# One decoder layer on one core: ScalarE writes the hidden layer's high part and full value, instead of ScalarE and VectorE in turn

## The chip, the cores and the metric

The kernel runs on 1 core of a Trainium2 chip. The time is device microseconds (µs) of one execution of the whole program. TensorE does the matrix products, ScalarE (ACT) the activations, VectorE (DVE) and GpSimd (POOL) elementwise work and reductions, SyncE (SP) issues the transfers.

## What is computed

For 16 batches of 256 tokens, each 256 wide: `x + attention(layernorm(x))` with 16 heads, then a cross attention to 77 context rows, then a soft mixture layer. All in float32. The mixture layer, which the change touches, is

```
logits   = xn @ se.T                     # 256 tokens x 1024 slots (8 experts x 128)
slots    = softmax over tokens (logits).T @ xn
h        = gelu(slots @ w1)              # 1024 slots x 1024 hidden, exact gelu
processed= h @ w2
out      = softmax over slots (logits) @ processed
```

## The kernel before

Products that need float32 accuracy are made of three products of rounded numbers (function `three`, lines 456 to 460): an operand is split into a high part, rounded to float32r, and a low part, the rest; the sum is hi·hi + lo·hi + hi·lo. So each intermediate result is split: as a rule ScalarE copies it out of PSUM rounded (`_hi`) and VectorE subtracts this from the same bank (`_lo`, `minus`, L1060).

The hidden layer is split in another way. Four chunks of 256 slots are worked one after the other in each batch; in a chunk TensorE makes four quarters (`hidden`, 12 products each, into one PSUM bank: banks 6 and 5 in turn, banks 1 to 4 in the last batch), ScalarE evaluates gelu of a quarter into the float32 tile `h_f` (`ge`, L1006), VectorE rounds it into `h_hi` (`hid`, L1278), and GpSimd subtracts: `h_lo = h_f - h_hi` (`hid` of its own, L1396). `h_lo` and `h_f` lie in the same memory, so the subtraction is in place. A quarter is 128x512 elements. The product with `w2` (`outer`, two halves of 24 products) of a chunk starts when the fourth `h_lo` is there. The semaphore `ge` is also what TensorE waits for before it writes the bank again: `hidden` of quarter 2 and 3, the transposes `lt` of the next chunk (bank 6), `slots` (bank 5).

A batch passes three stages, called c (self attention), d (cross attention) and m (mixture; l is the last chunk of the batch before). Each pass of the main loop holds c of batch b+2, d of b+1 and m of b. The order of the steps on each engine is written out by hand in lists of tokens such as `m.hidden.0.3` (stage, step, chunk, quarter): START, ORDER (the loop body, 13 passes, b = 1 to 13) and FINISH. An engine does its list strictly in order; semaphores tie the engines together. MISC and QUAD (with _START and _FINISH) say in which order the steps of c and d use PSUM bank 0 and banks 1 to 4. `idle` steps in START are products that nobody reads, put between waits.

Exp (`ed`, `ec`, `ex`, `ex2`) and gelu (`ge`) lie in different activation tables, so ScalarE loads a table whenever its list goes from one to the other. The copies need no load.

Steps named below: `mh2`, `xo`, `pr`, `cb`, `sl`, `ds` are ScalarE's copies out of PSUM; `mx` is VectorE's maximum over four banks (L1141), `sh` its mask subtraction, `nrm` its normalisation, `acc` its sum of the output (L1296), `edn` its normalisation of the dispatch weights. On TensorE `lt`, `dispatch`, `comb`, `mt`, `tr`, `ob` are transposes, `scores`, `shifted`, `pv` (L546, L566 with L570, L583) work on 32-row or 32-column parts of the array, `combine` and `slots` are products of the `three` kind.

Of the kernel before, what the change touches and what calls it, by code (L numbers as in the profile page):

```python
# [14 lines left out]
G, R, Q, C = 4, 4, 4, 2  # L15
# [73 lines left out]
        d0.scores2.1 d0.pv2.0 c1.k d0.mt2.1 c1.q d0.shifted2.1 d0.tr2.0 c1.v d0.ob2.0 c1.scores.0 d0.pv2.1 s1.idle.3
        d0.tr2.1 s1.idle.4 c1.mt.0 s1.idle.4 d0.ob2.1 c1.shifted.0 d0.oproj2 s1.idle.1 c1.scores.1 c1.pv.0 s1.idle.6  # L90
        c1.mt.1 s1.idle.5 c1.shifted.1 s1.idle.3 d0.xt.3 s1.idle.7 d0.logits.0 d0.logits.1 d0.logits.2 d0.logits.3
        s1.idle.3 m0.lt.0 c1.scores.2 c1.pv.1 s1.idle.6 c1.mt.2 s1.idle.2 m0.dispatch.0 c1.shifted.2 c1.tr.0
        m0.slots.0 c1.ob.0 c1.scores.3 c1.pv.2 m0.hidden.0.0 c1.mt.3 m0.hidden.0.1 c1.shifted.3 d1.kv m0.hidden.0.2
# [1465 lines left out]
```

## Time and profile before

| | |
|---|---|
| three runs | 1810.91, 1811.00, 1812.59 µs; median 1811.0 |
| profiled execution, its own time | 1810.3 µs |
| its span, first to last instruction | 1808.5 µs |
| TensorE busy | 1781.7 µs |
| VectorE busy | 1062.4 µs |
| ScalarE busy | 970.0 µs |
| GpSimd busy | 429.9 µs |

The profile is of one execution. Engine rows give busy time; a busy TensorE is one whose products overlap in its pipeline, so where exactly it loses time is read from the starts of its products in the timeline. A chain of waits is followed back from the last instruction. Times in the timeline count from the first instruction.

### The profile page before, as it was taken

What the parts mean: (1) busy time and instruction counts of PE and PEld (TensorE: products, weight loads), DVE (VectorE), ACT (ScalarE), POOL (GpSimd) and SP (SyncE); (2) the same over time, 40 slices, a digit from 0 to 9 for tenths busy, and PEclk for the clock granted to TensorE, in tenths of its full rate; (3) what the DMA queues carried; (4) which work ended last, traced back from release to release, by engine and by line L of the source; (5) the groups of instructions that cost most, each with busy time, mean ns of one, the idle gap of its engine ahead of it and who ended that gap; (6) DMA issues with size and microseconds to landing.
All of it is one profiled execution on the core that took longest, in us unless ns stands there. A gap on an engine that the chain in (4) does not pass through costs nothing.

```text
span 1808.5 us, 40567 instructions
## 1 busy us (share of the span) xinstructions
PE 1781.7 (99%) x17278; PEld 1596.0 (88%) x17278; DVE 1062.4 (59%) x2213; ACT 970.0 (54%) x1713; POOL 429.9 (24%) x351
## 2 busy tenths in 40 slices
...
DMA packets 20851, 19.65 MB, mean 11 GB/s; under 512 B 9921, under 2 KB 19777, under 8 KB 20289
## 3 DMA queue, kind: packets, MB, share of 16 engines
...
q14 instruction: 41, 0.33, 0.1%
...
## 4 chain that ended last, share of the span: by engine, by line
PE 91%; DVE 4%; POOL 3%; ACT 2%; issue 1%; DMA 0%; POOLq 0%; DVEq 0%; SPq 0%; ACTq 0%
PE ps L458 22%; PE ps L459 20%; PE ps L460 20%; PE ps L546 4%; PE ps L566 3%; POOL h_lo L1396 3%; PE ps L583 2%; PE ps L677 2%; PE ps L693 2%; PE ps L836 2%; PE ps L658 2%; PE ps L768 1%; PE ps L613 1%; PE ps L759 1%; PE ps L500 1%; DVE h_hi L1278 1%
## 5 line engine op out<-in xcount | busy, mean ns | idle before, releaser
L1396 POOL TENSOR_TENSOR h_lo<-h_f,h_hi 128x512 fp32r<-128x512 f32 x256 | 336.2, 1323 | 1125.8 <-DVE h_hi L1278 1125.8
L458 PE MATMUL ps<-w_hi,h_hi 128*128 128x256 f32 x1024 | 299.4, 292 | 6.4 <-POOL h_lo L1396 4.6
L458 PE MATMUL ps<-sl_hi,w_hi 128*128 128x256 f32 x1024 | 302.4, 295 | 1.9 <-DVE sl_lo L1060 1.5
L459 PE MATMUL ps<-w_hi,h_lo 128*128 128x256 f32 x1024 | 289.3, 283 | 0.0
L459 PE MATMUL ps<-sl_hi,w_lo 128*128 128x256 f32 x1024 | 289.2, 282 | 0.0
L460 PE MATMUL ps<-sl_lo,w_hi 128*128 128x256 f32 x1024 | 289.1, 282 | 0.0
L460 PE MATMUL ps<-w_lo,h_hi 128*128 128x256 f32 x1024 | 289.1, 282 | 0.0
L1006 ACT ACTIVATE h_f<-ps 128x512 f32<-128x512 f32 x256 | 149.4, 597 | 143.0 <-PE ps L460 142.4
L1278 DVE CAST h_hi<-h_f 128x512 fp32r<-128x512 f32 x256 | 156.7, 622 | 118.0 <-ACT h_f L1006 117.6
L458 PEld LDWEIGHTS ps<-w_hi,h_hi 128*128 128x128 f32 x1024 | 195.1, 191 | 21.5 <-POOL h_lo L1396 18.5
L458 PEld LDWEIGHTS ps<-sl_hi,w_hi 128*128 128x128 f32 x1024 | 195.0, 190 | 20.2 <-issue 10.5
L459 PEld LDWEIGHTS ps<-sl_hi,w_lo 128*128 128x128 f32 x1024 | 195.7, 191 | 0.1
L459 PEld LDWEIGHTS ps<-w_hi,h_lo 128*128 128x128 f32 x1024 | 195.5, 191 | 0.0
L460 PEld LDWEIGHTS ps<-sl_lo,w_hi 128*128 128x128 f32 x1024 | 195.5, 191 | 0.0
L460 PEld LDWEIGHTS ps<-w_lo,h_hi 128*128 128x128 f32 x1024 | 195.4, 191 | 0.0
L910 ACT ACTIVATE pt<-ps 128x2048 f32<-128x2048 f32 x64 | 120.4, 1881 | 81.5 <-PE ps L570 72.9
L1141 DVE TENSOR_REDUCE mx<-ps 128x8 f32<-128x2048 f32 x64 | 146.2, 2285 | 22.5 <-PE ps L546 22.4
L1060 DVE TENSOR_TENSOR ds_lo<-ps,ds_hi 128x512 fp32r<-128x512 f32 x64 | 44.1, 688 | 90.5 <-ACT ds_hi L879 90.4
L879 ACT ACTIVATE ds_hi<-ps 128x512 fp32r<-128x512 f32 x64 | 38.2, 597 | 104.3 <-PE ps L768 104.2
L970 ACT ACTIVATE edt<-ps,cm 128x256 f32<-128x256 f32 x128 | 59.6, 470 | 60.6 <-DVE cm L1257 58.9
L1006 ACT ACT_TABLE_LOAD x67 | 86.0, 1283 | 8.7 <-PE ps L460 7.6
L879 ACT ACTIVATE mh<-ps 128x512 fp32r<-128x512 f32 (+1 forms) x96 | 43.9, 457 | 77.8 <-PE ps L555 54.6
...
## 6 DMA issues: line engine op xcount, KB each, us to landing
...
```

What stands on the lines that cost most here:

```text
L458: te.matmul(o, lhs[0], rhs[0], start=first, stop=False)
L459: te.matmul(o, lhs[1], rhs[0], start=False, stop=False)
L460: return te.matmul(o, lhs[0], rhs[1], start=False, stop=last)
L546: last = te.matmul(ps[:, 1 + i, t * S:(t + 1) * S], q[rows, c, t * P:(t + 1) * P], km[rows, e, c, :], start=True, stop=True)
L566: te.matmul(ps[:, 1 + i, j * S:(j + 1) * S], km[rows, e, c, j * P:(j + 1) * P], q[rows, c, :], start=True, stop=False)
L879: return nc.scalar.activation(o, i, ACT.Copy)
L910: nc.scalar.activation(pt[:, :, :, :].rearrange("p i j s -> p i (j s)"), ps[:, 1:1 + R, :], ACT.Exp)\
L970: last = nc.scalar.activation(edt[:, e, :], ps[:, 6, e * S:(e + 1) * S], ACT.Exp, bias=cm[:, k:k + 1], accum_out=csum[:, k:k + 1])
L1006: nc.scalar.activation(h_f[:, 2 * q:2 * q + 2, :], halves(hidden_bank(b, q)), ACT.Gelu).then_inc(s["ge"], 1)
L1141: V.tensor_reduce(mx[:, n, :, :], ps[:, 1:1 + R, :].rearrange("p i (t s) -> p i t s", t=NT), AX, ALU.max, negate=True).then_inc(s["mx"], 1)
L1278: V.tensor_copy(h_hi[:, 2 * q:2 * q + 2, :], h_f[:, 2 * q:2 * q + 2, :]).then_inc(s["h_hi"], 1)
L1396: Q_.tensor_tensor(h_lo[:, part, :], h_f[:, part, :], h_hi[:, part, :].bitcast(f32), ALU.subtract)\
```

## The change

Three things. ScalarE's `ge` evaluates gelu twice from the same bank: first rounded into `h_hi`, then in full into `h_f`; `ge` is signalled by the second, `h_hi` by the first. VectorE's `hid` is gone. GpSimd's `hid` waits for both. The lists of START and ORDER, and MISC and MISC_START, are new; the lists of FINISH are as before, but VectorE's without `hid`. VectorE's `kv` waits in addition for `pv2` of the batch before.

```diff
             def ge(b, c, q):   # ScalarE
-                nc.scalar.activation(h_f[:, 2 * q:2 * q + 2, :], halves(hidden_bank(b, q)), ACT.Gelu).then_inc(s["ge"], 1)
+                part = slice(2 * q, 2 * q + 2)
+                nc.scalar.activation(h_hi[:, part, :], halves(hidden_bank(b, q)), ACT.Gelu).then_inc(s["h_hi"], 1)
+                nc.scalar.activation(h_f[:, part, :], halves(hidden_bank(b, q)), ACT.Gelu).then_inc(s["ge"], 1)
             def kv(a):         # VectorE
                 dve.wait_ge(s["kv_ps"], nth("kv_ps", a, 1))
+                if later(a):
+                    dve.wait_ge(s["pv2"], nth("pv2", a - 1, C))
-            def hid(b, c, q):  # VectorE
-                n = 4 * c + q
-                dve.wait_ge(s["ge"], nth("ge", b, n + 1))
-                V.tensor_copy(h_hi[:, 2 * q:2 * q + 2, :], h_f[:, 2 * q:2 * q + 2, :]).then_inc(s["h_hi"], 1)
             def hid(b, c, q):  # GpSimd
                 pool.wait_ge(s["h_hi"], nth("h_hi", b, 4 * c + q + 1))
+                pool.wait_ge(s["ge"], nth("ge", b, 4 * c + q + 1))
```

TensorE's list of the loop (ORDER), before and after:

```diff
-        m.lt.0 l.outer.3.0 d.kv m.dispatch.0 l.outer.3.1 c.xt.1 l.comb.3 m.slots.0 d.xt.2 c.k c.q m.hidden.0.0 d.q2
-        c.v m.hidden.0.1 d.scores2.0 m.hidden.0.2 m.hidden.0.3 d.mt2.0 m.lt.1 l.combine.3 d.shifted2.0 m.outer.0.0
-        m.dispatch.1 c.scores.0 d.pv2.0 m.comb.0 m.slots.1 m.outer.0.1 c.mt.0 m.hidden.1.0 c.shifted.0 m.hidden.1.1
-        d.tr2.0 d.scores2.1 c.pv.0 m.hidden.1.2 m.hidden.1.3 d.mt2.1 m.lt.2 m.combine.0 d.shifted2.1 d.ob2.0
-        m.outer.1.0 m.dispatch.2 c.scores.1 d.pv2.1 m.slots.2 m.comb.1 c.mt.1 m.outer.1.1 m.hidden.2.0 c.shifted.1
-        m.hidden.2.1 d.tr2.1 c.scores.2 m.combine.1 d.ob2.1 m.hidden.2.2 c.mt.2 m.hidden.2.3 m.lt.3 d.oproj2
-        c.shifted.2 c.pv.1 m.outer.2.0 c.tr.0 m.dispatch.3 c.scores.3 c.pv.2 m.slots.3 m.comb.2 c.mt.3 m.outer.2.1
-        d.xt.3 c.shifted.3 m.hidden.3.0 m.hidden.3.1 c.pv.3 d.logits.0 c.ob.0 m.hidden.3.2 m.hidden.3.3 c.tr.1
-        d.logits.1 d.logits.2 d.logits.3 c.ob.1 m.combine.2 c.oproj
+        m.lt.0 l.outer.3.0 d.kv m.dispatch.0 l.outer.3.1 c.xt.1 m.slots.0 l.comb.3 c.k d.xt.2 c.q m.hidden.0.0 d.q2
+        c.v m.hidden.0.1 d.scores2.0 m.hidden.0.2 m.hidden.0.3 d.mt2.0 m.lt.1 l.combine.3 d.shifted2.0 m.outer.0.0
+        m.dispatch.1 c.scores.0 d.pv2.0 m.slots.1 m.comb.0 c.mt.0 m.outer.0.1 c.shifted.0 m.hidden.1.0 m.hidden.1.1
+        d.tr2.0 d.scores2.1 c.pv.0 m.hidden.1.2 d.mt2.1 m.hidden.1.3 m.lt.2 m.combine.0 d.shifted2.1 m.outer.1.0
+        m.dispatch.2 c.scores.1 d.ob2.0 m.outer.1.1 c.mt.1 m.slots.2 m.comb.1 d.pv2.1 c.shifted.1 d.tr2.1
+        m.hidden.2.0 m.hidden.2.1 c.pv.1 c.scores.2 m.hidden.2.2 m.hidden.2.3 c.mt.2 m.lt.3 m.combine.1 c.tr.0
+        c.shifted.2 d.ob2.1 m.outer.2.0 m.dispatch.3 c.pv.2 c.scores.3 d.oproj2 m.slots.3 m.comb.2 c.mt.3 m.outer.2.1
+        c.ob.0 c.shifted.3 m.hidden.3.0 m.combine.2 m.hidden.3.1 d.xt.3 m.hidden.3.2 m.hidden.3.3 c.pv.3 d.logits.0
+        d.logits.1 c.tr.1 d.logits.2 c.ob.1 d.logits.3 c.oproj
```

ScalarE's list of the loop after:

```
        m.ed.0 m.ds.0 c.xt.1 l.cb.3 l.pr.3 m.sl.0 d.xt.2 d.q2 c.q m.ge.0.0 m.ge.0.1 m.ge.0.2 d.mh2.0 m.ge.0.3 m.ed.1
        d.ex2.0 m.ds.1 m.ec.0 d.xo2.0 m.sl.1 m.cb.0 c.mh.0 c.ex.0 m.ge.1.0 m.ge.1.1 c.xo.0 m.pr.0 m.ge.1.2 d.mh2.1
        m.ge.1.3 m.ed.2 d.ex2.1 m.ec.1 m.ds.2 d.od2.0 c.mh.1 m.cb.1 m.sl.2 d.xo2.1 c.ex.1 m.ge.2.0 c.xo.1 m.ge.2.1
        m.pr.1 m.ge.2.2 c.mh.2 m.ge.2.3 m.ed.3 c.ex.2 m.ec.2 d.od2.1 m.ds.3 c.xo.2 m.sl.3 m.cb.2 c.mh.3 m.pr.2 c.od.0
        c.ex.3 m.ge.3.0 m.ge.3.1 d.xt.3 m.ge.3.2 m.ge.3.3 c.xo.3 m.ec.3 d.logits.0 d.logits.1 c.od.1 d.logits.2
        d.logits.3
```

In both versions this list loads a table eight times in a pass (four times to gelu, four times back). VectorE's list of the loop after has, around the steps spoken of below, `c.k m.row_max c.v d.mx2.0`, `c.mx.0 m.sl.1 m.cb.0 c.sh.0` and `m.cm.3 c.sh.2 c.nrm.0 m.acc.1 m.edn.3`. Through the whole program the new ScalarE list changes table 129 times, the old one 135 times; the difference lies in START. START has 184 idle products after and 183 before.

## Rows read from the trace of the kernel before

**Rows 1.** The page, part 1: busy time, share, instructions of each engine.
```profile
PE 1781.7 (99%) x17278; PEld 1596.0 (88%) x17278; DVE 1062.4 (59%) x2213; ACT 970.0 (54%) x1713; POOL 429.9 (24%) x351
```

**Rows 2.** Busy time by stage: start:end, length, busy (instructions) by engine, PE clock.
```profile
0.00:233.00 233.00, 220.70 (x2194) 187.39 (x2195) 124.60 (x261) 117.65 (x188) 46.85 (x43) 1.00 0.12 35
341.10:449.10 108.00, 107.86 (x1057) 96.75 (x1056) 65.43 (x137) 59.21 (x105) 25.96 (x21) 1.00 0.03 7
1637.80:1808.50 170.70, 158.05 (x1357) 150.50 (x1355) 87.27 (x171) 82.16 (x160) 45.14 (x35) 1.00 0.02 6
```

**Rows 3.** Chain that ended last: start, length, what (same place, first and last pass).
```profile
308.86 2.64 POOL h_lo L1396 x2
...
1605.60 2.64 POOL h_lo L1396 x2
```

**Rows 4.** Waits of TensorE's weight loads in 233 to 1638: total, times, longest.
```profile
PEld ps L458 <- POOL h_lo L1396: 12.0, 26, 0.6
```

**Rows 5.** The page, part 5: groups, busy and mean, idle before and releaser.
```profile
L1396 POOL TENSOR_TENSOR h_lo<-h_f,h_hi 128x512 fp32r<-128x512 f32 x256 | 336.2, 1323 | 1125.8 <-DVE h_hi L1278 1125.8
...
L1006 ACT ACTIVATE h_f<-ps 128x512 f32<-128x512 f32 x256 | 149.4, 597 | 143.0 <-PE ps L460 142.4
L1278 DVE CAST h_hi<-h_f 128x512 fp32r<-128x512 f32 x256 | 156.7, 622 | 118.0 <-ACT h_f L1006 117.6
...
L1006 ACT ACT_TABLE_LOAD x67 | 86.0, 1283 | 8.7 <-PE ps L460 7.6
```

**Rows 6.** Tile h_hi: VectorE's rounding, duration min/median/max in ns.
```profile
L1278 DVE CAST h_hi<-h_f x256: 411/427/1427, 133.7 to 1791.7; 128x512 fp32r<-128x512 f32 x128
```

**Rows 7.** Timeline of TensorE in a pass of the loop: start, length, what.
```profile
846.91 0.29 PE L460 MATMUL ps<-sl_lo,w_hi 128*128 128x256 f32 x1
847.03 0.60 PE L759 MATMUL ps<-consts,lg 128*128 128x128 f32 x4
...
850.60 1.07 PE L583 MATMUL ps<-pt,vz 128*32 128x256 f32 x16
851.82 0.39 PE L458 MATMUL ps<-w_hi,h_hi 128*128 128x256 f32 x1
...
856.84 1.07 PE L583 MATMUL ps<-pt,vz 128*32 128x256 f32 x16
857.84 0.39 PE L458 MATMUL ps<-ds_hi,xs_hi 128*128 128x256 f32 x1
...
864.35 0.48 PE L570 MATMUL ps<-sh,ones 32*128 32x256 f32 x4
864.76 0.39 PE L458 MATMUL ps<-sl_hi,w_hi 128*128 128x256 f32 x1
```

**Rows 8.** Timeline of ScalarE, the same pass and the program's end.
```profile
832.90 0.60 ACT L879 ACTIVATE sl_hi<-ps 128x512 fp32r<-128x512 f32 x1 [0.99 <-PE ps L460]
...
842.37 1.09 ACT L1006 ACTIVATE h_f<-ps 128x512 f32<-128x512 f32 x2
...
847.23 0.60 ACT L1006 ACTIVATE h_f<-ps 128x512 f32<-128x512 f32 x1 [0.57 <-PE ps L460]
...
1791.02 0.60 ACT L1006 ACTIVATE h_f<-ps 128x512 f32<-128x512 f32 x1 [0.84 <-PE ps L460]
```

**Rows 9.** Timeline of VectorE, the same pass.
```profile
842.34 2.29 DVE L1141 TENSOR_REDUCE mx<-ps 128x8 f32<-128x2048 f32 x1 [0.33 <-PE ps L546]
...
846.61 0.82 DVE L1278 CAST h_hi<-h_f 128x512 fp32r<-128x512 f32 x1
```

**Rows 10.** Timeline of GpSimd, the same pass and the program's end.
```profile
845.85 1.30 POOL L1396 TENSOR_TENSOR h_lo<-h_f,h_hi 128x512 fp32r<-128x512 f32 x1 [20.30 <-DVE h_hi L1278]
847.51 1.27 POOL L1396 TENSOR_TENSOR h_lo<-h_f,h_hi 128x512 fp32r<-128x512 f32 x1 [0.36 <-DVE h_hi L1278]
...
1791.65 2.79 POOL L1396 TENSOR_TENSOR h_lo<-h_f,h_hi 128x512 fp32r<-128x512 f32 x2 [0.36 <-DVE h_hi L1278]
```

**Rows 11.** Timeline of TensorE at the program's end.
```profile
1794.48 0.39 PE L458 MATMUL ps<-w_hi,h_hi 128*128 128x256 f32 x1 [2.07 <-POOL h_lo L1396]
```

More of the change, by code:

```diff
@@ L89 @@
[L89 to L93, printed above, removed]
@@ L94 @@
-        s1.idle.1 c1.pv.3 s1.idle.2 c1.tr.1 m0.hidden.0.3 c1.ob.1 m0.lt.1 c1.oproj m0.outer.0.0 m0.dispatch.1 d1.xt.2
-        m0.outer.0.1 c2.xt.1 m0.slots.1 m0.comb.0 c2.k c2.q c2.v m0.hidden.1.0 c2.scores.0 d1.q2 m0.hidden.1.1
-        c2.mt.0 m0.hidden.1.2 c2.shifted.0 m0.hidden.1.3 d1.scores2.0 c2.pv.0 m0.lt.2 d1.mt2.0 m0.combine.0
-        d1.shifted2.0 m0.outer.1.0 m0.dispatch.2 d1.scores2.1 d1.pv2.0 m0.outer.1.1 d1.mt2.1 m0.slots.2 m0.comb.1
-        d1.shifted2.1 d1.tr2.0 m0.hidden.2.0 d1.ob2.0 c2.scores.1 m0.hidden.2.1 m0.hidden.2.2 c2.mt.1 m0.hidden.2.3
@@ L99 @@
-        d1.pv2.1 c2.shifted.1 m0.lt.3 d1.tr2.1 m0.combine.1 d1.ob2.1 c2.scores.2 c2.pv.1 m0.dispatch.3 d1.oproj2
-        m0.comb.2 c2.mt.2 m0.slots.3 c2.shifted.2 m0.outer.2.0 c2.tr.0 c2.scores.3 c2.pv.2 m0.outer.2.1 c2.mt.3
-        m0.hidden.3.0 c2.shifted.3 d1.xt.3 m0.hidden.3.1 m0.hidden.3.2 m0.combine.2 c2.pv.3 d1.logits.0 c2.ob.0
-        m0.hidden.3.3 c2.tr.1 d1.logits.1 d1.logits.2 c2.ob.1 d1.logits.3 c2.oproj
+        s0.idle.1 s0.se_transp.0.0 s0.idle.3 c0.mt.2 s0.idle.4 c0.shifted.2 c0.tr.0 s0.idle.3 c0.ob.0 s0.idle.1
@@ new lines @@
+        c0.scores.3 c0.pv.2 s0.se_transp.0.1 s0.idle.4 c0.mt.3 s0.idle.4 c0.shifted.3 s0.idle.8 c0.pv.3 s0.idle.2
+        c0.tr.1 s0.se_transp.1.0 s0.idle.2 c0.ob.1 s0.idle.2 c0.oproj s0.idle.3 d0.kv s0.idle.8 d0.xt.2 s0.idle.5
+        d0.q2 s0.se_transp.1.1 s0.idle.2 d0.scores2.0 c1.xt.1 s0.idle.6 d0.mt2.0 c1.k d0.shifted2.0 s0.idle.8
+        d0.scores2.1 d0.pv2.0 s0.idle.3 d0.mt2.1 c1.q d0.shifted2.1 d0.tr2.0 c1.v c1.scores.0 d0.pv2.1 s1.idle.3
+        d0.ob2.0 s1.idle.2 c1.mt.0 s1.idle.4 c1.shifted.0 d0.tr2.1 s1.idle.3 d0.ob2.1 s1.idle.1 c1.scores.1 d0.oproj2
@@ new lines @@
+        s1.idle.5 c1.mt.1 s1.idle.6 c1.pv.0 s1.idle.4 d0.xt.3 c1.shifted.1 d1.kv d0.logits.0 d0.logits.1 d0.logits.2
+        d0.logits.3 s1.idle.3 c1.scores.2 c1.pv.1 m0.lt.0 s1.idle.4 c1.mt.2 s1.idle.4 c1.shifted.2 c1.tr.0
+        m0.dispatch.0 s1.idle.2 c1.ob.0 s1.idle.1 c1.scores.3 c1.pv.2 m0.slots.0 c1.mt.3 s1.idle.4 c1.shifted.3
+        m0.hidden.0.0 s1.idle.2 c1.pv.3 m0.hidden.0.1 c1.tr.1 m0.hidden.0.2 c1.ob.1 m0.hidden.0.3 c1.oproj m0.lt.1
+        m0.outer.0.0 m0.dispatch.1 m0.outer.0.1 c2.xt.1 m0.slots.1 c2.k c2.q c2.v d1.xt.2 m0.comb.0 c2.scores.0 d1.q2
@@ new lines @@
+        m0.hidden.1.0 c2.mt.0 c2.shifted.0 m0.hidden.1.1 m0.combine.0 d1.scores2.0 m0.hidden.1.2 d1.mt2.0
+        m0.hidden.1.3 m0.lt.2 d1.shifted2.0 c2.pv.0 m0.outer.1.0 d1.scores2.1 d1.pv2.0 m0.dispatch.2 d1.mt2.1
+        m0.comb.1 d1.shifted2.1 d1.tr2.0 m0.slots.2 d1.ob2.0 c2.scores.1 d1.pv2.1 m0.outer.1.1 c2.mt.1 m0.hidden.2.0
+        c2.shifted.1 m0.combine.1 d1.tr2.1 c2.scores.2 c2.pv.1 m0.hidden.2.1 m0.hidden.2.2 c2.mt.2 m0.hidden.2.3
+        d1.ob2.1 c2.shifted.2 d1.oproj2 m0.lt.3 m0.outer.2.0 c2.scores.3 m0.dispatch.3 c2.tr.0 m0.outer.2.1 c2.mt.3
@@ L103 @@
+        m0.slots.3 m0.comb.2 c2.pv.2 c2.shifted.3 d1.xt.3 m0.hidden.3.0 m0.combine.2 d1.logits.0 c2.ob.0
+        m0.hidden.3.1 m0.hidden.3.2 c2.pv.3 d1.logits.1 d1.logits.2 c2.tr.1 m0.hidden.3.3 c2.ob.1 d1.logits.3
+        c2.oproj
     """,
     act="""
-        c0.xt.1 s0.hi.0 s0.hi.1 c0.q c0.mh.0 c0.ex.0 s0.se_squares c0.xo.0 c0.mh.1 c0.ex.1 c0.xo.1 s0.hi.2 c0.mh.2
-        s0.hi.3 c0.ex.2 c0.od.0 s0.se_hi.0.0 c0.xo.2 c0.mh.3 c0.ex.3 s0.se_hi.0.1 c0.xo.3 s0.hi.4 c0.od.1
-        s0.se_hi.1.0 d0.xt.2 s0.se_hi.1.1 d0.q2 d0.mh2.0 d0.ex2.0 c1.xt.1 d0.xo2.0 d0.mh2.1 c1.q d0.ex2.1 d0.od2.0
@@ L187 @@
 MISC = """
-    d.kv c.xt1 d.xt2 d.q2 d.mt2.0 d.pv2.0 c.mt.0 d.tr2.0 c.pv.0 d.mt2.1 d.ob2.0 d.pv2.1 c.mt.1 d.tr2.1 d.ob2.1 c.mt.2
-    d.oproj2 c.pv.1 c.tr.0 c.pv.2 c.mt.3 d.xt3 c.pv.3 c.ob.0 c.tr.1 c.ob.1 c.oproj
+    d.kv c.xt1 d.xt2 d.q2 d.mt2.0 d.pv2.0 c.mt.0 d.tr2.0 c.pv.0 d.mt2.1 d.ob2.0 c.mt.1 d.pv2.1 d.tr2.1 c.pv.1 c.mt.2
+    c.tr.0 d.ob2.1 c.pv.2 d.oproj2 c.mt.3 c.ob.0 d.xt3 c.pv.3 c.tr.1 c.ob.1 c.oproj
 """.split()
```

100 lines of the change are left out of this document (44 added, 56 removed).

## The prediction

> **What bounds the kernel now.** I read the page's busy times first: TensorE 1781.7 of 1808.5 µs, ScalarE 970.0, VectorE 1062.4, GpSimd 429.9 [rows 1]. Busy time of overlapping products proves little, so next the stages and the chain. In the span's middle TensorE is busy 107.86 of 108.00 µs at clock 1.00, while at the start it lacks 12.3 of 233 µs and at the end 12.6 of 170.7 [rows 2]. The loop body repeats with a period of (1605.60 - 308.86) / 12 = 108.06 µs [rows 3], 13 times, 1404.8 µs of 1808.5. So the question is what 108.06 becomes, and then what the two ends become.
>
> GpSimd's 1125.8 µs of waiting for VectorE's rounding [rows 5] is the largest wait of the profile and costs almost nothing: TensorE's weight loads wait for `h_lo` 12.0 µs in 26 pieces over the 13 passes, two a pass [rows 4], and much of that lies behind products still in the array. What TensorE really loses is seen in its starts. A `pv` (16 L583) takes 1.00 from its start to the next step's when nothing is waited for (856.84 to 857.84), and 1.22 where `outer.2.0` follows (850.60 to 851.82) [rows 7]: 0.22 µs. `outer.1.0` loses 0.15 in the same way. That is 0.37 a pass, 4.8 in all, and all that the split of the hidden layer costs the loop.
>
> **Why that wait is there.** ScalarE has evaluated two quarters at 843.46 (842.37 + 1.09) [rows 8]; VectorE is in `mx` for 2.29 µs [rows 9], so GpSimd starts at 845.85 only, and its next one at 847.51: 1.66 apart though one takes 1.30 [rows 10]. The rounding between them is stretched to 0.82 [rows 9] against 0.41 undisturbed, and up to 1.43 [rows 6]. The Trainium skill has the reason ("SBUF — State Buffer", section "SBUF: two separate sides"): VectorE in a fast mode and GpSimd take a shared port pair as an exclusive lock. The rows agree (0.41 alone, up to 1.43 beside GpSimd). By that rule GpSimd's remaining subtractions still block VectorE's other fast operations, now at other moments.
>
> **The change part by part.**
>
> *VectorE's rounding goes.* 256 x 0.622 µs = 156.7 [rows 5], 8 to 10 µs of each pass's 65.43 [rows 2]. VectorE bounds nothing there, so this is worth nothing directly.
>
> *ScalarE evaluates twice.* Two evaluations back to back take 1.09, one 0.60 [rows 8], so the second costs 0.49. A rounded output costs the same as a plain one (`sl_hi` 0.60) [rows 8]. 16 x 0.49 = 7.8 µs a pass: 59.2 [rows 2] becomes 67.0, 62% of the pass; over the program 256 x 0.49 = 125. It bounds nothing on average either. No table load is added: both are gelu, and 67 loads of 1.28 [rows 5] stay or become a few less. Below: if the pair doesn't overlap it is 0.60, 9.6 a pass.
>
> *The way from a landed quarter to `h_lo`.* Before: 0.60, rounding 0.41 to 1.43 behind VectorE's queue, then GpSimd 1.30. After: 1.09, then 1.30, without VectorE. Alone that is 2.4 against 2.3 or more; its worth is that nothing of VectorE's queue stands in it, and that GpSimd's subtractions follow at 1.30, not 1.66. On the other hand `ge`, for which TensorE waits before it uses the bank again, comes 0.49 later, and all that stands behind `ge` in ScalarE's queue comes later by 0.49 for each quarter: `mh2`, `pr`, the table load ahead of `ed`.
>
> *The added wait of `kv` for `pv2`* looks back over more than 40 µs of the list (`pv2.1` stands in the middle of the pass, `kv` near the next one's start). It is free.
>
> *The new list of TensorE.* It has the same 90 steps. The steps cost the same wherever they stand, but the joints between them don't. From the last product of a step to the first of the next: 0.12 between full products and on to transposes (846.91 to 847.03), about 0.3 to 0.4 out of a 32-row step (0.41 over the last half's four short ones, 864.35 to 864.76) [rows 7]. Over the timeline each kind of joint repeats to 0.01: transposes to products 0.03, to transposes 0.11, to 32-row steps 0.20; products to 32-row steps 0.21; out of `scores` 0.30, of `pv` 0.31, of `shifted` 0.39; out of the projections `oproj` 0.22 to transposes, 0.31 to 32-row steps, 0.03 to products. Summed with these prices, the old list takes 107.42 without any wait. The pass takes 108.06; 0.37 are the waits above and 0.27 are hundredths spread over 90 joints. The new list changes 30-odd joints. Those that don't cancel: `oproj2` is followed by products, no longer by `shifted` (-0.28); two fewer transposes after transposes and one fewer 32-row step after them, for products after them (-0.36); two joints transposes to `pv` (+0.40, taken at 0.20 like the nearest, transposes to `scores`; between 0.11 and 0.31). With the small ones the new list sums to 107.05, range 106.9 to 107.3. Saved: 0.37.
>
> *Waits in the new loop.* I placed each chunk on the new list (µs from the pass's start, no waits; a quarter reaches ScalarE 0.32 after its last product starts, 846.91 to 847.23 [rows 7, 8]).
> Chunk 0: `hidden.0.2` is due at 20.94 and waits for `ge.0.0`, which stands behind `q2` and `q` (until 18.5), a table load (19.8) and its pair (20.95): 0.1 lost or none. `hidden.0.3`'s last product starts at 23.78; `mh2.0` stands ahead of `ge.0.3` and ends at 25.1, the pair at 26.2, GpSimd at 27.5; `outer.0.0` is due at 27.59. Nothing lost, 0.1 to spare.
> Chunk 1: `h_lo` at 51.3, due 51.90. Chunk 2: `h_lo` at 75.5, due 76.42; but `acc.1`, behind `sh.2` and `nrm.0` on VectorE, ends at 76.5: 0.1 lost. Chunk 3: `h_lo` at 100.4, due in the next pass.
> In sum 0.2 in place of 0.37. The other tight spots (2 µs between `hidden.c.2` and `lt`, a pair is through after 1.4) hold.
>
> The period: 107.05 + 0.27 + 0.2 = 107.5, against 108.06: -0.55, times 13 = -7.2 µs. Bounds: 107.2 (no waits) and 108.5 (0.25 lost at each of four chunks and the joints at their dear end): -11 to +6.
>
> *START.* Here latency of one batch's chain sets the time, and idle products fill it (184, before 183); QUAD_START, which orders that chain through banks 1 to 4, is unchanged. By prices the list is 0.3 shorter. The waits in it, 12.3 µs of TensorE not busy and more behind fillers [rows 2], fall elsewhere. Six table loads of 1.28 go [rows 5], off TensorE's path mostly. I take 0, bounds -4 and +4.
>
> *FINISH.* TensorE's and ScalarE's lists are the same, with 32 second evaluations in ScalarE's: 15.7 µs. At the very end it helps: the last evaluation starts 1791.02 [rows 8], its pair ends 1792.1, GpSimd is free and ends at 1793.5; before, its last two end at 1794.44 [rows 10], and `outer.3.0` starts 1794.48 after 2.07 idle [rows 11]. Gain 0.95. In chunks 0 to 2 of the last batch `ds` and `sl` stand behind one to three pairs, and reach TensorE 0.5 to 1.5 later; part of it goes into waits for `h_lo` already there. I take +0.5 for each of three, less 0.2 at the batch before. FINISH: +0.4; bounds -2 and +5.
>
> Sum: -7.2 + 0 + 0.4 = -6.8 on the profiled execution's own 1810.3 (span 1808.5 and 1.8 around it): 1803.5. The runs' median, 1811.0, is 0.7 above that execution: 1804.
>
> **Rivals.**
> *A, slower: ScalarE's queue becomes the wait in the loop.* The place is the gelu block of each chunk: table load, four pairs, and copies between them for which TensorE waits next. For it: only 0.1 is to spare at `outer.0.0` and none at `hidden.0.2`; at 0.60 for the second evaluation four pairs are 0.44 later. Against: 38% of ScalarE's pass remains idle. It decides when the waits exceed 1.1 a pass, 0.27 a chunk. At 1.6 a pass (0.4 a chunk) the period is 108.9: +11, and 1822. A page speaks for it: the Trainium skill ("ScalarE: Activation LUTs", section "Rules for kernel authors") gives plain elementwise work to VectorE, since it is faster there per element; the rows agree in size, 0.41 on VectorE and 0.49 on ScalarE. It would matter if ScalarE bounded.
> *B, no change: the joints don't pay.* The loop keeps new waits of 0.7 a pass and ends at 108.0; 1810 to 1811. For it: my prices come from one order, and the old list too had two tight spots.
> *C, faster by more.* No waits in the loop, and START gains 4: 13 x -0.85 - 4 = -15, 1796.
> *D, the change doesn't do what it says:* ScalarE would reload a table between the two evaluations, or the rounded one would be slower. Both are gelu, `sl_hi` shows the rounded form at full speed; 1 in 100.
>
> **How the numbers follow.** Forecast (1801 to 1807) 0.50, C 0.13, B 0.22, A 0.14, D 0.01. A measurement tells about 0.2%, 3.6 µs, from no change, so faster means below 1807.4, slower above 1814.6. Faster: forecast and C and a little of B, 0.65. Same: most of B and some of A, 0.21. Slower: 0.14. The range for 8 in 10 is 1796 to 1813; the likeliest case's own is 1801 to 1807.
>
> **What would show it.** The period by `outer.2.0` in successive passes: 107.5 (right), 108.0 (B), over 108.6 (A). GpSimd's subtractions back to back at 1.30, none 1.66 apart. ScalarE's pairs at 1.09 and about 67 µs busy in a pass, VectorE about 56. `outer.1.0` and `outer.2.0` without loss. TensorE's starts at the new joints: transposes to `pv` 0.20, `oproj2` to `slots` 0.03. At the end `outer.3.0` 1 µs sooner after its `combine.2`. I'd be wrong if START moved by more than 4 either way, or if `ds` and `sl` in the last batch cost over 1 µs each.

## The result, and the profile after

The changed kernel takes 1818.1 µs (median of 6 runs, 1817.1 to 1818.9) against 1811.0: ratio 1.0037, interval 1.0024 to 1.005. I had forecast a faster kernel, 1804 µs with a range of 1796 to 1813; the measured one is slower, and its time lies outside the range.

The profiled execution takes 1817.69 µs, of which the span is 1815.9. Line numbers of the changed kernel are 2 to 5 lower than those of the rows before (`h_lo` L1396 is L1392). The page's first part, as [rows 1]:

```profile
PE 1784.8 (98%) x17280; PEld 1599.7 (88%) x17280; DVE 942.8 (52%) x1957; ACT 1084.5 (60%) x1963; POOL 423.0 (23%) x351
```

VectorE lost 119.6 µs of work and ScalarE gained 114.5. Neither tells where the added 7.4 µs of span come from. The stages do, in the columns of [rows 2]:

```profile
0.00:242.40 242.40, 224.50 (x2197) 190.57 (x2198) 122.22 (x245) 117.44 (x198) 46.86 (x43) 0.98 0.11 34
350.20:458.20 108.00, 108.00 (x1059) 96.95 (x1058) 57.95 (x121) 66.92 (x121) 25.59 (x21) 1.00 0.03 7
1644.30:1815.90 171.60, 158.43 (x1357) 150.53 (x1355) 65.79 (x139) 96.70 (x192) 43.69 (x35) 0.99 0.02 6
```

The first and the last of these are START and FINISH; the bounds are the first product of the first loop pass and the first one after the last pass, in TensorE's timeline:

```profile
242.39 0.38 PE L755 MATMUL ps<-consts,lg 128*128 128x128 f32 x2
...
1644.28 0.38 PE L755 MATMUL ps<-consts,lg 128*128 128x128 f32 x2
```

A pass is (1644.28 - 242.39) / 13 = 107.84 µs. In the table, START runs from TensorE's first product of all (at 3.70 µs before, at 3.87 changed) to the first one of the loop; the whole is the median of the runs.

| kernel | START | a pass | FINISH | span | whole |
|---|---|---|---|---|---|
| before | 229.3 | 108.06 | 170.7 | 1808.5 | 1811.0 |
| changed | 238.5 | 107.84 | 171.6 | 1815.9 | 1818.1 |
| difference | +9.2 | -0.22 (13: -2.9) | +0.9 | +7.4 | +7.1 |

The three stages give +7.2; the span has 0.2 more since the first product itself comes 0.17 later. The loop did gain, less than forecast. START lost three times what the loop gained, and the first row above shows that TensorE's clock is no longer 1.00 there. Ten-microsecond stretches of START in the changed kernel, same columns:

```profile
60.00:70.00 10.00, 6.39 (x52) 5.84 (x50) 8.99 (x20) 1.44 (x3) 6.00 (x4) 0.96 0.16 38
70.00:80.00 10.00, 7.85 (x65) 7.52 (x66) 7.25 (x7) 0.60 (x1) 2.46 (x2) 0.53 0.01 2
80.00:90.00 10.00, 9.86 (x128) 8.21 (x126) 5.47 (x9) 4.33 (x5) 0.00 (x0) 1.00 0.01 2
```

TensorE is without work from 67.3 to 72.2 µs, and the clock granted from 70 to 80 is 0.53, about half. The timelines of the three engines there, changed kernel:

```profile
65.39 1.28 POOL L1385 TENSOR_TENSOR x<-x,biases 128x512 f32<-128x512 f32 x1
66.64 4.55 POOL L1423 TENSOR_TENSOR w_lo<-g_w,w_hi 128x2048 fp32r<-128x2048 f32 x1
71.42 1.27 POOL L1385 TENSOR_TENSOR x<-x,biases 128x512 f32<-128x512 f32 x1 [0.23 <-DVE xh_a L1104]
...
65.46 5.88 DVE L1104 TENSOR_SCALAR xh_a<-x,mv,pw 128x256 f32<-128x256 f32 x2
71.26 0.74 DVE L1349 SCALAR_TENSOR_TENSOR se_lo<-ps,gxs,se_hi 128x512 fp32r<-128x512 f32 x1
71.92 3.04 DVE L1335 SCALAR_TENSOR_TENSOR w_lo<-g_w,gam,w_hi 128x1024 fp32r<-128x1024 f32 x2
...
72.15 0.87 PE L853 MATMUL ps<-consts,g_se 128*128 128x128 f32 x3 [4.89 <-DVE se_lo L1349]
```

And the kernel before, GpSimd and VectorE:

```profile
55.88 4.53 POOL L1427 TENSOR_TENSOR w_lo<-g_w,w_hi 128x2048 fp32r<-128x2048 f32 x1 [18.15 <-ACT w_hi L879]
...
63.50 0.74 DVE L1354 SCALAR_TENSOR_TENSOR se_lo<-ps,gxs,se_hi 128x512 fp32r<-128x512 f32 x1
...
71.41 0.73 DVE L1106 TENSOR_SCALAR xh_a<-x,mv,pw 128x256 f32<-128x256 f32 x2
```

Read from the bottom up. TensorE waits 4.89 µs for `se_lo`. `se_lo` is queued on VectorE behind `c1.xh.1`, whose two `xh_a` instructions take 5.88 µs instead of 0.73, and end (71.34) just after GpSimd's `w_lo` ends (71.19). That is step `s0.lo.4`, w2's low part: the new GpSimd list has it behind `d0.bias.2`; in the old one it ran 10.8 µs earlier, and no VectorE instruction beside it took longer than it does alone. ScalarE's rounding of w2 and this subtraction moved, and have nothing to do with gelu. That the one holds up the other is so far only read from where they end; the runs below test it.

### The profile page after: what moved, and what is told of

It reads as the page before. It is cut to its first block, busy times and chain, and to the rows that moved or that the text cites. A ratio compares the mean times of both kernels' runs of the same rounds, so it can differ in the third digit from the quotient of the medians.

```text
span 1815.9 us, 40836 instructions
## 1 busy us (share of the span) xinstructions
PE 1784.8 (98%) x17280; PEld 1599.7 (88%) x17280; DVE 942.8 (52%) x1957; ACT 1084.5 (60%) x1963; POOL 423.0 (23%) x351
## 4 chain that ended last, share of the span: by engine, by line
PE 94%; DVE 2%; ACT 2%; POOL 1%; issue 1%; DMA 0%; POOLq 0%; DVEq 0%; SPq 0%; ACTq 0%
PE ps L454 21%; PE ps L455 20%; PE ps L456 20%; PE ps L562 4%; PE ps L542 4%; PE ps L579 3%; PE ps L673 2%; PE ps L689 2%; PE ps L719 2%; PE ps L654 2%; PE ps L764 1%; PE ps L609 1%; PE ps L755 1%; PE ps L832 1%; PE ps L496 1%; PE ps L861 1%
## 5 line engine op out<-in xcount | busy, mean ns | idle before, releaser
L1392 POOL TENSOR_TENSOR h_lo<-h_f,h_hi 128x512 fp32r<-128x512 f32 x256 | 330.8, 1300 | 939.3 <-ACT h_f L1004 938.4
L1003 ACT ACTIVATE h_hi<-ps 128x512 fp32r<-128x512 f32 x256 | 153.5, 600 | 63.9 <-PE ps L456 63.2
L1004 ACT ACTIVATE h_f<-ps 128x512 f32<-128x512 f32 x256 | 153.7, 600 | 0.0
L1375 POOL TENSOR_TENSOR pw_d<-ve_d,consts 128x2 f32<-128x2 f32 (+1 forms) x32 | 27.5, 859 | 264.8 <-DVE ve_d L1082 264.8
```

Source lines behind the costliest of these rows:

```text
L1003: nc.scalar.activation(h_hi[:, part, :], halves(hidden_bank(b, q)), ACT.Gelu).then_inc(s["h_hi"], 1)
L1004: nc.scalar.activation(h_f[:, part, :], halves(hidden_bank(b, q)), ACT.Gelu).then_inc(s["ge"], 1)
L1392: Q_.tensor_tensor(h_lo[:, part, :], h_f[:, part, :], h_hi[:, part, :].bitcast(f32), ALU.subtract)\
```

## The experiments

**Theory:** GpSimd's moved subtraction holds VectorE's `xh_a`, TensorE starves, its clock falls; this is START's loss. **Rivals:** the new START order is longer by itself; the second evaluation is what START pays for; in the loop and in FINISH, ScalarE's queue.

START repeats within 1.2 µs between kernels that have the same START (229.3, 229.1, 228.1 for the old order and split; 232.7, 232.4, 232.3 for that of run 1), so single tenths of it are not read. Part of that is there early: `d0.xt.2` starts 59.6 to 60.2 µs after TensorE's first product in kernels that are alike up to it. Waits are idle times of TensorE as the timeline gives them in brackets.

### 1. w2's low part back at its old place
```
POOL  - c0.bias.1 d0.rstd.2 c1.rstd.1 d0.bias.2 s0.lo.4 c1.bias.1
      + c0.bias.1 s0.lo.4 d0.rstd.2 c1.rstd.1 d0.bias.2 c1.bias.1
ACT   - c0.xo.3 s0.se_hi.1.0 c0.od.1 s0.hi.4
      + c0.xo.3 s0.hi.4 s0.se_hi.1.0 c0.od.1
```


> The changed kernel with one step of START put back where it stood before: GpSimd's subtraction for w2's low part (s0.lo.4) ahead of d0.rstd.2 instead of behind d0.bias.2, and ScalarE's rounding of w2 (s0.hi.4), which feeds it, ahead of s0.se_hi.1.0. Everything else is the changed kernel. Theory 1 (the 9.4 us that START lost come from that subtraction: it now runs at 66.64 to 71.19 beside VectorE's xh_a at 65.46, which takes 5.88 us instead of 0.73, TensorE then waits 4.89 us for se_transp.1.1 and works the next 10 us at a granted clock of 0.53): xh_a takes 0.7 us again, no idle time of TensorE of over 1 us between 60 and 90 us, granted clock 1.00 there, m.lt.0 of the first loop pass starts at about 234 instead of 242.39, and the whole takes 1809.5 us (1808.5 to 1811). Rival (the new START order is longer by itself, whatever GpSimd does): at least 1814 us. In between would mean that both have a part.

Measured: 1811.7 µs (1810.6 to 1812.4), ratio to before 1.0001 (0.9993 to 1.001); START 232.7, a pass 107.83. GpSimd and VectorE in this kernel:

```profile
66.12 1.28 POOL L1385 TENSOR_TENSOR x<-x,biases 128x512 f32<-128x512 f32 x1
...
66.19 1.69 DVE L1104 TENSOR_SCALAR xh_a<-x,mv,pw 128x256 f32<-128x256 f32 x2
```

Two steps moved back, the subtraction (it now runs at 56.26 to 60.78) and the rounding that feeds it, return 5.8 µs of START and 6.4 of the whole. The clock in 70 to 80 µs is 1.00. `xh_a` is still 1.69, not 0.7: it now meets GpSimd's `x += bias`, 1.28 µs, and waits for that one. The time is above the theory's 1808.5 to 1811 and below the rival's 1814: both have a part, and START is still 3.4 above the kernel before. Which of the two moves did it this run can't tell; run 2 leaves both where the changed kernel has them, and changes the subtraction alone.

### 2. The same subtraction in four pieces, at its new place
```
-  Q_.tensor_tensor(low, src, hi.bitcast(f32), ALU.subtract)
+  for k in range(4): Q_.tensor_tensor(low[:, 2*k:2*k+2, :], ...)
```


> The changed kernel with its orders untouched; GpSimd's subtraction for w2's low part is issued as four of 128x512 (of some 1.3 us each by the 128x512 ones of the trace) instead of one of 128x2048 (4.55 us). Theory 1 (a GpSimd elementwise instruction holds VectorE's fast fp32 forms off for as long as it runs, and lets them in where it ends): xh_a beside it takes 1.3 to 3.5 us instead of 5.88, se_transp.1.1 waits 2.5 to 4.5 us less, START is 2 to 5 us shorter than the 238.5 of the changed kernel, the whole 1813 to 1816 us. Rival 1 (VectorE waits for the whole of GpSimd's work on w2, by a semaphore or by buffers): xh_a still 5.9 us, or longer as four pieces cost more than one, the whole 1818 to 1819 us. Rival 2 (a loss of bandwidth instead of a lock: xh_a is slow for as long as GpSimd moves data): again 5.9 us or more.

Measured: 1815.8 µs, START 236.3 (-2.2). VectorE and GpSimd:

```profile
65.67 2.64 DVE L1104 TENSOR_SCALAR xh_a<-x,mv,pw 128x256 f32<-128x256 f32 x2
68.24 0.74 DVE L1349 SCALAR_TENSOR_TENSOR se_lo<-ps,gxs,se_hi 128x512 fp32r<-128x512 f32 x1
68.90 3.83 DVE L1335 SCALAR_TENSOR_TENSOR w_lo<-g_w,gam,w_hi 128x1024 fp32r<-128x1024 f32 x2
...
66.84 7.01 POOL L1425 TENSOR_TENSOR w_lo<-g_w,w_hi 128x512 fp32r<-128x512 f32 x4
```

The first `xh_a` ends behind `x += bias`, the second behind the first piece: 2.64 instead of 5.88. So VectorE is held for one GpSimd instruction at a time. The price comes after: the four pieces take 7.01 instead of 4.55, and VectorE's own `w_lo`, with two operands in SBUF, 3.83 instead of 3.04. `se_transp.1.1` waits 1.65 for `se_lo`, 3.2 less, and `d0.mt2.0` behind it waits 2.44 more. START, the whole and `xh_a` lie where the theory put them; neither rival's values came.

### 3. Fillers in the wait
```
PE  - d0.q2 s0.se_transp.1.1 s0.idle.2
    + d0.q2 s0.idle.24 s0.se_transp.1.1 s0.idle.2
```


> The changed kernel with 24 idle products (each a 128x128 by 128x128 product into a spare bank, as START has them everywhere) put between d0.q2 and s0.se_transp.1.1, so that TensorE works through the time in which it now waits for se_lo. VectorE's 5.88 us xh_a stays. Theory 1 as for e1, in two parts: some 5 us are the wait and some 3.3 us are the half clock after it. Filling the wait keeps the clock up, so the products of 72 to 79.5 us run at full speed: 1815 us (1814 to 1816), granted clock of 70 to 80 us at 0.9 or more. Rival 1 (the clock falls there for another reason than the idle time): 1818 us, clock still about 0.53. Rival 2 (the products themselves are late): 1818 us or more.

Measured: 1817.3 µs (1816.0 to 1817.6), START 237.9. The time is not the 1814 to 1816 that I expected. The granted clock is:

```profile
70.00:80.00 10.00, 9.36 (x109) 8.76 (x110) 8.53 (x9) 1.78 (x3) 3.07 (x2) 1.00 0.00 1
```

With work in the wait the clock stays at 1.00, so it was the idle time that brought it down. But of the 3.3 µs that I had expected from it only 1.7 are seen at `c1.x1` (VectorE's `x` at 145.42, changed kernel 147.12), and 0.6 at START's end. The fillers overran the wait by 0.3, and at `c2.xt.1` TensorE is idle 0.91 behind a load of `x`, 4.18 µs on its way; that the idle products already in the list absorbed the rest is my reading. This execution was also 0.6 late before the first filler (`d0.xt.2` at 64.04 instead of 63.47). So the half clock is worth 0.6 to 2.3 µs; START's own spread of 1.2 allows no closer value. Most of the 5.8 is the wait (4.89 before `se_transp.1.1`, 0.70 in run 1).

### 4. `se_lo` ahead of `xh_a` on VectorE
```
DVE - c1.stats.1 d0.xt.2 c1.xh.1 s0.se_lo.1.0 s0.lo.3
    + c1.stats.1 d0.xt.2 s0.se_lo.1.0 c1.xh.1 s0.lo.3
```


> The changed kernel with one swap in VectorE's START order: s0.se_lo.1.0 (0.74 us, reads PSUM) ahead of c1.xh.1 (the xh_a that takes 5.88 us beside GpSimd's 4.55 us subtraction). GpSimd's order and its subtraction at 66.64 to 71.19 stay. Theory 1 (GpSimd's instruction holds off only the fast form on SBUF operands, as xh_a has it, and TensorE suffered since se_lo was queued behind it): se_lo takes 0.7 us at about 65.5, se_transp.1.1 waits under 0.3 us, no fall of the clock, START 233 to 235 us (238.5 in the changed kernel), the whole 1812 to 1814. Rival 1 (every VectorE instruction is slow beside it): se_lo takes 4 us or more, the wait stays, 1818. Rival 2 (xh_a, now later, makes c1.xt.1 late instead): START 237 or more.

Measured: 1817.4 µs, START 238.6. VectorE, GpSimd, TensorE:

```profile
65.38 0.74 DVE L1349 SCALAR_TENSOR_TENSOR se_lo<-ps,gxs,se_hi 128x512 fp32r<-128x512 f32 x1
66.04 5.34 DVE L1104 TENSOR_SCALAR xh_a<-x,mv,pw 128x256 f32<-128x256 f32 x2
...
65.41 1.29 POOL L1385 TENSOR_TENSOR x<-x,biases 128x512 f32<-128x512 f32 x1
66.65 4.57 POOL L1423 TENSOR_TENSOR w_lo<-g_w,w_hi 128x2048 fp32r<-128x2048 f32 x1
...
71.52 0.63 PE L496 MATMUL ps<-consts,xh_a 128*128 128x128 f32 x4 [2.00 <-DVE xh_a L1104]
...
76.99 1.11 PE L663 MATMUL ps<-consts,md 128*128 128x128 f32 x4 [2.85 <-DVE xa_lo L1058]
```

Rival 2 is right on the time, theory 1 on the mechanism. `se_lo`, which reads PSUM, takes 0.74 beside GpSimd's `x += bias`; `xh_a` is held until 71.38, 0.15 after `w_lo` ends. The wait moved on to the transposes of `xh_a` and to `md`, in the same size (2.00 and 2.85 against 4.89), and the clock with it (0.63 in 70 to 80 µs). VectorE's whole chain is 5 µs late; swapping inside it doesn't help.

### 5. The old START order, double evaluation kept
START and MISC_START of the kernel before, less VectorE's `hid` steps; the rest is the changed kernel.

> The changed kernel (gelu evaluated twice, new loop and FINISH orders) with the START orders of the kernel before on all four engines, less VectorE's rounding steps. Theory 1 (START's order lost 9.4 us, the loop gained 2.9, FINISH lost 0.9): START takes 229 to 230 us as before, the loop 107.84 a pass, the whole 1808.7 us (1807.5 to 1810). Rival (the second gelu evaluation in START, 12 of 0.49 us on ScalarE, is what moved START): START at 232 us or more and the whole at least 1811 us.

Measured: 1810.6 µs, ratio 0.9997 (0.9988 to 1.0006); START 231.0, a pass 107.84, span 1808.2. START is between the theory's 230 and the rival's 232, and the whole is above the theory's 1807.5 to 1810: under the old order the double evaluation costs START 1.7 (230.5 in run 6, so 1.2 by that one), seen as waits before `d1.mt2.0` and `d1.scores2.0` (0.90 and 0.65, before 0.30 and 0.35).

### 6. The split alone, under all the old orders
The changed functions; START, ORDER, FINISH and MISC of the kernel before, less `hid`.

> The changed functions alone (gelu twice on ScalarE, no rounding on VectorE) under all the orders of the kernel before, less VectorE's rounding steps. It tells what the double evaluation is worth without any reordering. Theory 1 (TensorE stays the bound, the pass only loses small waits): START 229 to 230 us, a loop pass between 107.7 and 108.1, FINISH between 170.7 and 173, the whole 1807 to 1812 us. Rival (the doubled gelu of 0.5 us more a pair delays ScalarE's copies where the order was made for single ones, so that the reordering was needed): a loop pass of 108.5 us or more, and the whole at 1816 us or more.

Measured: 1822.6 µs, ratio 1.0062 (1.0049 to 1.0074); START 230.5, a pass 108.77, FINISH 171.6. The rival holds: without the new order the double evaluation makes a pass 0.71 longer. A pass in this kernel:

```profile
348.35:457.12 108.77, 108.41 (x1059) 96.85 (x1058) 57.06 (x122) 66.58 (x121) 25.23 (x22) 1.00 0.03 7
```

### 7. The new loop order with the old split
The functions of the kernel before, its START and FINISH; ORDER and MISC new, VectorE's 16 `hid` steps put in by hand (`... c.v m.hid.0.0 d.mx2.0 m.hid.0.1 m.hid.0.2 d.sh2.0 m.hid.0.3 m.cm.1 ...`).

> The loop orders of the changed kernel with the functions of the kernel before (one gelu a quarter on ScalarE, VectorE rounds it), VectorE's 16 rounding steps put by hand into its new order where their gelu ends; START and FINISH as in the kernel before. With the old order and the double evaluation a pass took 108.77 us, with both new 107.84, with both old 108.06. Theory 1 (the new order is better by itself, the double evaluation costs something on ScalarE in either order): a pass of 107.8 or less, the whole 1809 us or less. Rival (the new order only works since VectorE has the 13 us a pass free): 108.3 us or more a pass and 1814 us or more; a place of mine that is badly chosen would look the same, and shows as one large wait for h_lo or for a VectorE step in the pass.

Measured: 1833.9 µs, ratio 1.0126 (1.0112 to 1.014); a pass 109.81. TensorE in a pass:

```profile
859.85 0.39 PE L458 MATMUL ps<-w_hi,h_hi 128*128 128x256 f32 x1 [0.66 <-POOL h_lo L1398]
```

This wait for `h_lo` is in every pass (8.6 µs in 13), as are waits for VectorE's `sh` and `on` (4.4 each). That is what the rival and a badly chosen place both look like, and the run doesn't part them. Together with run 6: old order and old split 108.06, old order and double evaluation 108.77, both new 107.84. So the double evaluation needs the new order. Whether the new order needs the double evaluation stays open: the 109.81 may be my placing.

### 8. A third evaluation, in the loop
```
+  if 0 < b < B - 2: nc.scalar.activation(scr[q % 2], halves(hidden_bank(b, q)), ACT.Gelu)
```
on top of run 1, between the other two, into a spare tile.

> The first experiment (changed kernel with w2's low part at its old place) with a third gelu evaluation of each quarter from the same bank into a spare tile, in the 13 passes of the loop alone: 16 times 0.49 us, 7.8 us more of ScalarE a pass (from 66.9 to 74.8 of 107.8). It doubles the cost that the change adds. Theory (ScalarE's latency already sets some of the waits of a pass, with the changed order tuned for two): a pass 0.5 to 1.5 us longer than 107.84, the waits before outer.0.0 to outer.3.0 and before the products behind ScalarE's copies, the whole 1818 to 1831. Rival 1 (ScalarE has slack, as its busy share of 62% suggests; TensorE covers it): a pass 107.9 or less, the whole 1812.5 or less. Rival 2 (ScalarE becomes the chain): 3 us or more a pass, 1850 or more.

Measured: 1831.5 µs; a pass 109.37 (+1.54) for 7.1 µs more of ScalarE:

```profile
342.00:451.37 109.37, 108.43 (x1058) 96.95 (x1057) 56.60 (x121) 74.00 (x138) 25.68 (x21) 1.00 0.03 7
```

The growth is just above the theory's 0.5 to 1.5, and far from both rivals. The waits are before `hidden.0.2` (for `h_f`, 6.2 µs in the 13 passes) and for `h_lo` before `outer.0.0` (5.6). ScalarE, busy 62% of a pass, has no free slack in this order: each microsecond more of it costs 0.2 here, and cost 0.1 under the old order in run 6 (0.71 for 7.4). No order made for three evaluations was tried.

### 9. GpSimd's bias step away from `h_lo`
In the loop `d.bias.2` ahead of `m.hid.1.0` instead of ahead of `m.hid.2.3`, on top of run 1.

> The first experiment (w2's low part back at its old place) and one more move, in the loop: GpSimd's x += bias for the cross attention (d.bias.2, 1.28 us) ahead of m.hid.1.0 instead of between m.hid.2.2 and m.hid.2.3, where the product outer.2.0 waits 0.13 us behind it. Theory 1 (of the 0.34 us a pass that the forecast missed, 0.13 are this wait): a pass of 107.70 instead of 107.84, the whole 1.7 us below the first experiment, 1810 us. Rival (the wait is for ScalarE's pair in any case, or the bias step now meets a VectorE instruction and holds it): 107.84 or more a pass, 1811.7 us or more.

Measured: 1811.7 µs, a pass 107.86. It gained nothing: the rival's time, though for neither of its reasons. GpSimd, VectorE and TensorE in this kernel:

```profile
957.82 1.27 POOL L1392 TENSOR_TENSOR h_lo<-h_f,h_hi 128x512 fp32r<-128x512 f32 x1 [0.66 <-ACT h_f L1004]
...
959.31 0.68 DVE L1291 TENSOR_TENSOR acc<-ps,acc 128x512 f32<-128x512 f32 x1
...
960.13 0.36 PE L454 MATMUL ps<-w_hi,h_hi 128*128 128x256 f32 x1
```

The last `h_lo` is there 1.04 before `outer.2.0` starts (0.50 before it in the changed kernel), and the product still starts 0.16 after the last one of `d.ob2.1`, where this joint has 0.03 without a wait. `outer` waits for VectorE's `acc` as well, and `acc.1` ends 0.15 before `outer.2.0` starts, in both kernels and in each of the passes 4, 7 and 11. So the 0.13 are a wait for `acc.1`, as the prediction had it for chunk 2 (0.1). This is read from the code and the starts; no run moved `acc.1`.

### 10. Steps moved in START and FINISH
On top of run 9.

```
ACT START   c2.mh.0 c2.ex.0 m0.ec.1        (was m0.ec.1 c2.mh.0 c2.ex.0)
PE  START   m0.hidden.1.3 d1.mt2.0         (was d1.mt2.0 m0.hidden.1.3)
ACT FINISH  ds.1, sl.2, ds.3, pr.1, sl.3 ahead of gelu pairs
```


> As the one with d.bias.2 moved, and with five more steps moved, after the waits of the changed kernel. START: ScalarE's c2.mh.0 and c2.ex.0 ahead of m0.ec.1 (0.97 us, behind which c2.shifted.0 waits 1.09), TensorE's m0.hidden.1.3 ahead of d1.mt2.0 (which waits 1.28). FINISH: for the last batch ScalarE's copies ds.1, sl.2, ds.3, pr.1, sl.3 ahead of gelu pairs (slots.1 waits 1.40, hidden.2.0 0.94, slots.3 0.59, hidden.3.0 0.58). Theory (each of these waits is ScalarE's queue, not a chain that moves along): START 2 us less, FINISH 1.5 to 2.5 us less, the whole 1806 us (1805 to 1808). Rival (the waits return at the next product that needs the delayed gelu): FINISH within 0.5 us of 171.6, the whole 1809 us or more.

Measured: 1812.2 µs; START 233.7 (232.4 in run 9), FINISH 171.6. The rival holds for FINISH. `slots.1` waits 0.25 instead of 1.24, and in exchange there are waits before `comb.0` (0.52), `outer.1.0` (0.97) and `outer.2.0` (1.31) of which the changed kernel has none over 0.25. In the last batch a turn in ScalarE's queue is paid by a later product. START got no shorter either: `c2.shifted.0` still waits 0.99, and `hidden.1.2` now waits 1.08 and `d1.shifted2.0` 1.03.

### 11. Double evaluation in the loop alone
`ge` evaluates twice only for batches 1 to 13; START and FINISH are those of the kernel before with VectorE's `hid`; ORDER and MISC are new.

> Double evaluation and new order only in the 13 passes of the loop; START and FINISH with the orders of the kernel before and with its split (one gelu a quarter, VectorE rounds). Theory (the stages add up: START 229.3 and FINISH 170.7 as before, a pass 107.84): span 1805.6 us, 2.9 below the kernel before, the whole 1808 us (1807 to 1809.5) against 1811, ratio 0.9984. The double evaluation then costs 1.6 us in START and 0.9 in FINISH, which is what the kernel with the old START order showed. Rival (at the seams the loop's new order meets a state that the old START leaves, and gives back some of it): 1810 us or more, a first pass longer than 108 us.

Measured: 1807.5 µs (1806.8 to 1808.7), against 1810.6 for the kernel before in the same session: ratio 0.9985 (0.9976 to 0.9994), span 1805.6:

```profile
0.00:232.80 232.80, 220.48 (x2195) 187.12 (x2196) 125.68 (x261) 117.68 (x188) 46.90 (x43) 1.00 0.11 35
340.60:448.45 107.85, 107.85 (x1057) 96.82 (x1056) 57.94 (x121) 66.97 (x121) 25.61 (x21) 1.00 0.03 7
1634.80:1805.60 170.80, 158.02 (x1357) 150.49 (x1355) 88.31 (x171) 82.15 (x160) 44.91 (x35) 0.99 0.02 6
```

The stages add up to the forecast 1805.6: the two ends as before [rows 2], the loop as changed. This version is faster than the kernel before by 3 µs, and than the changed one by 10.

### 12. The new START order with the old split
Run 11 with the START of run 1, the 16 rounding steps of batch 0 put in by hand.

> As the one with the double evaluation in the loop alone, but with the new START order (w2's low part at its old place), with VectorE's 16 rounding steps of the first batch put by hand into it. It tells apart what of START's remaining 3.4 us (232.7 in the first experiment against 229.3) is the order and what the double evaluation, which cost 1.6 us under the old order. Theory 1 (the new START order is longer by itself): START 231 to 233 us. Rival (it is the double evaluation): START 229 to 230 us, the whole as the mixed kernel. A badly chosen place of a rounding step would show as a wait for h_lo of over 0.5 us at an outer product of batch 0.

Measured: 1813.3 µs, START 234.6, of which two waits are of my placing (`outer.0.0` 1.34, in run 1 0.30; `c2.ob.1` 1.50, there none): 232.1 without them, by subtraction and not by a run. But the two largest waits that run 1 has in START from 70 µs on are here too, with one evaluation: `c2.shifted.0` 0.99 (run 1: 0.99) and `d1.mt2.0` 1.45 (1.12); the kernel before has 0.30 or less at both. They come with the order, also without the second evaluation. That speaks for the order being longer by itself; by how much isn't settled.

**START's 9.2 µs in sum.** 5.8 for w2's low part (run 1). The other 3.4 are the second evaluation and the new order, and their shares are no better known than START repeats: 1.7 and 1.7 if the second evaluation costs what it did under the old order (run 5), 0.6 and 2.8 by run 12. Beside the two waits just named, run 1 has 0.70 before `se_transp.1.1` and 0.84 before `d0.mt2.0`, both behind VectorE; the kernel before has no such wait at either. No run took any of these waits away by itself.

## Why the prediction was wrong

**START at 0, bounds -4 to +4: this is the step that failed, and it decides the sign.** "Idle products fill it", I wrote, and "the waits in it ... fall elsewhere", without walking the new lists of GpSimd, VectorE and ScalarE. It measured +9.2, more than twice my upper bound. The fillers that I trusted are a fixed number between two steps; they cover no wait that wasn't there when they were counted. The prediction even wrote, with the Trainium skill ("SBUF — State Buffer", section "SBUF: two separate sides"), that GpSimd's subtractions would block VectorE's fast operations "at other moments", and then put no price on it. It thought of the 1.3 µs ones only. The longest GpSimd instruction of the kernel, 4.53 µs, was in the trace, and its step had moved in GpSimd's list. That section of the Trainium skill calls the pair an exclusive lock for a whole instruction; the rows agree: the two `xh_a` take 0.73 alone, 1.69 beside 1.28, 2.64 beside 1.28 and a piece of 1.33, 5.88 beside 1.28 and 4.55 one after the other.

**The loop: right in direction, 0.22 instead of 0.55 a pass, so 2.9 µs of gain instead of 7.2.** ScalarE's pairs took 1.09 as forecast, its pass 66.9 (67), VectorE's 57.95 (56), and GpSimd's subtractions follow the pairs. In the page's groups:

```profile
L1392 POOL TENSOR_TENSOR h_lo<-h_f,h_hi 128x512 fp32r<-128x512 f32 x256 | 330.8, 1300 | 939.3 <-ACT h_f L1004 938.4
...
L1003 ACT ACTIVATE h_hi<-ps 128x512 fp32r<-128x512 f32 x256 | 153.5, 600 | 63.9 <-PE ps L456 63.2
...
L1004 ACT ACTIVATE h_f<-ps 128x512 f32<-128x512 f32 x256 | 153.7, 600 | 0.0
```

The weight loads' waits for `h_lo` fell from 12.0 in 26 [rows 4] to:

```profile
PEld ps L454 <- ACT h_f L1004: 5.4, 13, 0.4
...
PEld ps L454 <- POOL h_lo L1392: 3.9, 13, 0.3
```

The first is `hidden.0.2` behind `ge.0.0`, foreseen at 0.1 or none: most of it lies behind products in the array, and the product starts 0.05 later than with single evaluation in the same order (run 7). With 0.13 at `outer.2.0` (run 9), and 0.03 or less at two more, the waits are 0.2 a pass, as I had them.

**What failed in the loop is the sentence "The steps cost the same wherever they stand".** The timeline of TensorE, cut into steps by the lists, gives for all 90 (medians of 11 passes, so the sums can miss a pass by 0.01):

| kernel | steps, first to last product | joints, waits in them | a pass |
|---|---|---|---|
| before | 92.98 | 15.07 | 108.06 |
| changed | 93.25 | 14.59 | 107.84 |
| difference | +0.27 | -0.48 | -0.22 |

The joints and waits gave 0.48 of the 0.54 that I had summed. The steps took 0.27 back, for which the sum had nothing. The quarter `hidden.1.3`, first and last product, before (behind `hidden.1.2`) and changed (behind `d.mt2.1`):

```profile
928.22 0.28 PE L458 MATMUL ps<-sl_hi,w_hi 128*128 128x256 f32 x1
...
929.54 0.28 PE L460 MATMUL ps<-sl_lo,w_hi 128*128 128x256 f32 x1
```
```profile
936.72 0.36 PE L454 MATMUL ps<-sl_hi,w_hi 128*128 128x256 f32 x1
...
938.11 0.28 PE L456 MATMUL ps<-sl_lo,w_hi 128*128 128x256 f32 x1
```

That is 1.32 and 1.39 for the same 12 products. So the cheap joint of 0.03 from transposes to products is paid for inside the step behind it, and so is a joint out of a 32-row step; both kernels have it alike:

| step | behind full products | behind transposes | behind 32-row steps |
|---|---|---|---|
| `hidden` | 1.32 | 1.39 to 1.40 | 1.40 to 1.42 |
| `outer` | 2.76 | 2.83 to 2.85 | 2.85 to 2.86 |
| `logits` | 1.13 to 1.15 | 1.24 to 1.25 | 1.26 |

The joint on which I counted most, `oproj2` to `slots.3`, did fall by 0.28; but `oproj2` grew from 1.51 to 1.62, behind `scores` instead of transposes, and `slots.3` from 1.41 to 1.50. What the 0.27 was that the old list took beyond my prices isn't shown.

**Rival A was real, hidden by the order.** It had 0.14. Runs 6 and 8 show that ScalarE's queue does cost the loop (0.71 and 1.54); the new order of the pass makes up for the 0.71 and 0.22 more. So the second evaluation by itself isn't free, though "It bounds nothing on average" let it look so.

**FINISH +0.4: it measured +0.9.** The end gained what I said: `outer.3.0` starts after 1.15 idle, 2.07 before [rows 11]:

```profile
1801.89 0.38 PE L454 MATMUL ps<-w_hi,h_hi 128*128 128x256 f32 x1 [1.15 <-POOL h_lo L1392]
```

The chunks before it cost 1.8 in sum, where I had 1.3; the clearest is `slots.1`, with 0.55 more than before at:

```profile
1750.50 0.39 PE L454 MATMUL ps<-ds_hi,xs_hi 128*128 128x256 f32 x1 [1.24 <-DVE ds_lo L1058]
```

Runs 6 and 11 place the 0.9 on the second evaluation: 171.6 with the old lists and double, 170.8 with single.
